# Layer-norm statistics of five tiles taken by ScalarE and GpSimd, and context statistics placed behind the scan

## The reference

```
x = x + attn(layernorm(x))          # 1024 -> 128, four layers, -> 1024
x = x + xattn(layernorm(x), ctx)    # top-k channel mask and pooling
x = x + ffn(layernorm(x))           # top 2 of 8 experts, 1024 x 1024 each

# attn, each layer: y = silu(ln(h)); y = sconv(y) (a complex recurrence over the
#   sequence); h = h + y*scale; y = ln(h); h = h + W2 silu(W1 y + b1) + b2
# xattn: mask = top 154 of 256 entries of ctx along the sequence, per channel
#   crucial = mask*x, rest = (1-mask)*x; max and mean of both over the sequence,
#   a 7-tap convolution over the channels, a norm, a sigmoid: two gates
#   out = crucial*gate1 + rest*gate2
# ffn: the two best experts per row, weighted with a softmax of their logits
```

## Time and profile before

| | |
|---|---|
| median of 3 runs | 1062.95 us (1062.17 to 1064.01) |
| the profiled execution | 1063.64 us, span 1061.8 us |
| mean granted TensorE clock | 0.964 |
| busy: TensorE, VectorE, ScalarE, GpSimd | 985.7, 537.7, 383.2, 463.1 us |
| block 1 | 0 to 351 us |
| pooling (block 3) | 353 to 441 us |
| gates, residual, routing | 441 to 538 us |
| expert products | 538 to the end |

### The profile page before, as it was taken

The page is one execution under the profiler, slowest core; times in us unless marked ns, Lnnn a source line. Parts: engine busy times, 40 slices in busy tenths (PEclk is TensorE's granted clock), DMA queues, the critical chain, the costliest instruction groups (busy, mean ns, idle before and its releaser), DMA issues. The chain is left out here.

```text
span 1061.8 us, 13204 instructions
## 1 busy us (share of the span) xinstructions
PE 985.7 (93%) x3508; PEld 518.5 (49%) x3515; DVE 537.7 (51%) x1547; ACT 383.2 (36%) x1032; POOL 463.1 (44%) x567
## 2 busy tenths in 40 slices
PE   6888999999999797999299999999999999999995
PEld 5786556566554453355144444444444444444442
DVE  5548899999988799789832111111111111111111
ACT  2436889899873487488300000000000000000000
POOL 3664766766750100087153344444434333333341
PEclk9989999999999898999579999999999999999997
DMA  7520120200004300037676643737346373463332
GB/s 290 173 75 1 51 91 11 90 1 2 1 1 159 140 21 1 1 141 285 253 259 192 211 106 79 237 79 237 77 132 175 68 230 72 107 205 79 79 79 40
DMA packets 38462, 120.25 MB, mean 113 GB/s; under 512 B 6220, under 2 KB 9351, under 8 KB 38408
## 3 DMA queue, kind: packets, MB, share of 16 engines
q1 hardware_dynamic: 25592, 79.77, 20.6%
q0 software_dynamic: 12816, 39.86, 16.8%
HBM read 82.91 MB, written 36.70 MB: 113 GB/s over the span
## 5 line engine op out<-in xcount | busy, mean ns | idle before, releaser
L2106 PE MATMUL bank<-T,X 128*128 x1184 | 510.2, 594 | 0.8 <-DVEq L2156 0.8
L2106 PEld LDWEIGHTS bank<-T,X 128*128 128x128 f32 x1184 | 225.6, 191 | 285.5 <-issue 285.5
L2154 DVE TENSOR_SCALAR X<-bank,col_p 128x512 f32<-128x512 f32 x37 | 27.8, 750 | 386.7 <-PE bank L2106 386.7
L2127 ACT ACTIVATE X<-bank,col_p 128x512 f32<-128x512 f32 x37 | 25.4, 687 | 493.8 <-PE bank L2106 493.8
L2066 POOL DMA_INDIRECT out_dram<-X,col_d x37 | 60.0, 1622 | 261.0 <-DVE X L2154 244.8
L2057 POOL DMA_INDIRECT X<-x_nrm,col_s x152 | 145.7, 959 | 51.3 <-issue 46.2
L490 POOL TENSOR_TENSOR rs<-ve,neg_half 128x4 f32<-128x4 f32 x36 | 52.9, 1470 | 55.1 <-DVE ve L979 55.1
L849 ACT ACTIVATE M<-X,T 128x256 bf16<-128x256 f32 x152 | 75.1, 501 | 0.0
L665 PE MATMUL bank<-nat,T 128*128 128x512 f32 x128 | 62.8, 612 | 3.4 <-DVE ve L979 2.0
L1502 DVE STREAM_TRANSPOSE X<-X 128x1024 f32<-128x1024 f32 x39 | 48.4, 1240 | 33.1 <-DMA X<-x_nrm,col_s 30.2
L673 PE MATMUL bank<-X,T 128*128 128x512 f32 x128 | 60.6, 602 | 0.0
(11 more groups left out here) (341 smaller groups left out, 1407.8 us busy)
## 6 DMA issues: line engine op xcount, KB each, us to landing
T<-in_L_ffn_expert_w_dram SPq DMA_DIRECT2D x8, 4096.0 KB, 17.6
out_dram<-X SPq DMA_DIRECT2D x17, 512.0 KB, 5.9
M<-in_x_dram SPq DMA_DIRECT2D x16, 512.0 KB, 7.6
X<-in_x_dram SPq DMA_DIRECT2D x16, 512.0 KB, 5.9
x_nrm<-H SPq DMA_DIRECT2D x16, 512.0 KB, 3.8
T<-in_ctx_dram SPq DMA_DIRECT2D x9, 512.0 KB, 3.6
X<-x_nrm,col_s POOLq DMA_INDIRECT x152, 3.7
X<-in_ctx_dram SPq DMA_DIRECT2D x4, 512.0 KB, 7.0
```

What stands on the lines that cost most here:

```text
L2106: mm = nc.tensor.matmul(bank[2 * u + n][:, :], xgt[u][:, k, :], Tf[:, ds(odd * D + (k * N + n * BANK), BANK)], start=(k == 0), stop=(k == ...
```

## The change

- **Statistics of tiles 0 to 4.** `rows` of these tiles now also sums each half row (`accum_out`). GpSimd makes the mean of the two sums (`squared_mean`); ScalarE squares the two halves of the row with the mean as its bias and sums them (`squared_tile`); GpSimd adds the two sums, multiplies by 1/1024 and adds epsilon (`squared_var`), then takes the power. All of this is in block 1. VectorE takes no statistics of tiles 0 to 4 any more, neither those of tiles 0 and 1 in block 1 nor those of tiles 2 to 4 in block 3.
- **Context statistics.** In slots up to 2 `stats` stands behind `scan` instead of at the head of the slot.
- Three semaphores are merged into others, the `spill` buffer is made earlier, and `sums` has one more wait, for the squares that wrote the same buffers.

```diff
         def counted(m, t):
-            return m * NT + t + 1 - (sum(...) if m == 1 else 0)
+            if m == 0:
+                return t + 1 - sum(i in SQUARED for i in range(t + 1))
+            return NT - len(SQUARED) + t + 1 - sum(on_scalar(*divmod(i, CT)) for i in range(t + 1))
...
         def rows(act, t):
             for n in range(2):
+                from_bank = bank[2 + 2 * (t % 2) + n][:, :]
+                if t in SQUARED:
+                    if SQUARED.index(t) >= 4:
+                        hold(act, sq_var, 2 * (SQUARED.index(t) - 4) + 2)
+                    hold(act, o2_mm, 2 * t + n + 1)
+                    nc.scalar.activation(X[:, t, n * BANK:(n + 1) * BANK], from_bank, ACT.Copy, accum_out=sum_at(t, n)).then_inc(x1_done, 1)
...
+        def squared_mean(pool, t):
+            pool.wait_ge(x1_done, 2 * t + 2)
+            nc.gpsimd.tensor_scalar(mean_of(0, t), sum_at(t, 0), sum_at(t, 1), 1.0 / D, ALU.add, ALU.mult).then_inc(sq_mean, 1)
+
+        def squared_tile(act, t):
+            k = SQUARED.index(t)
+            if k > 0:
+                hold(act, sq_sum, k)
+            hold(act, sq_mean, k + 1)
+            for n in range(2):
+                ins = nc.scalar.activation(wide_junk[n], X[:, t, n * BANK:(n + 1) * BANK], ACT.Square, scale=-1.0, bias=mean_of(0, t),
+                                           accum_out=sum_at(t, 2 + n))
+            ins.then_inc(sq_sum, 1)
+
+        def squared_var(pool, t):
+            k = SQUARED.index(t)
+            var = ve_all(0)[:, t:t + 1]
+            pool.wait_ge(sq_sum, k + 1)
+            nc.gpsimd.tensor_tensor(var, sum_at(t, 2), sum_at(t, 3), ALU.add).then_inc(sq_var, 1)
+            pool.wait_ge(sq_var, 2 * k + 1)
+            nc.gpsimd.tensor_scalar(var, var, 1.0 / D, EPS, ALU.mult, ALU.add).then_inc(sq_var, 1)
+            pool.wait_ge(sq_var, 2 * k + 2)
...  # GpSimd, end of block 1
-                for t in range(CT):
+                squared_mean(pool, 0)
+                for t in range(FIRST_TILES):
+                    if t + 1 < FIRST_TILES:
+                        squared_mean(pool, t + 1)
+                    squared_var(pool, t)
                     ln_pow(pool, 0, t)
...  # ScalarE, end of block 1
                 for t in range(FIRST_TILES):
                     rows(act, t)
+                    if t > 0:
+                        squared_tile(act, t - 1)
+                squared_tile(act, FIRST_TILES - 1)
...  # VectorE, a slot of block 1
-                    if b1 is not None:
+                    if b1 is not None and s > 2:
                         stats(b1, h1)
...
                     if 0 <= s + 1 < VISITS:
                         scan(s + 1)
+                    if b1 is not None and s <= 2:
+                        stats(b1, h1)
...  # VectorE, end of block 1
-                for t in range(CT):
-                    hold(dve, x1_done, 2 * t + 2)
-                    ln_stats(dve, 0, t)
...  # block 3: GpSimd, ScalarE's sums, VectorE
-                for t in range(CT, NT):
+                for t in range(FIRST_TILES, NT):
                     ln_pow(pool, 0, t)
...
+                    hold(act, sq_sum, sum(t < FIRST_TILES or t - 1 <= n + LAG + 1 for t in SQUARED))
...
-                    if CT <= t < NT:
+                    if t < NT and t not in SQUARED:
```

More of the change, by code:

```diff
@@ L217, in on_scalar, with sum_at @@
             return b >= FIRST_SQUARED and h == 0
+        SQUARED = list(range(FIRST_TILES))
         def counted(m, t):
-            return m * NT + t + 1 - (sum(on_scalar(*divmod(i, CT)) for i in range(t + 1)) if m == 1 else 0)
+            if m == 0:
+                return t + 1 - sum(i in SQUARED for i in range(t + 1))
+            return NT - len(SQUARED) + t + 1 - sum(on_scalar(*divmod(i, CT)) for i in range(t + 1))
+        def sum_at(t, k):
+            return back_of(0, 4 * (SQUARED.index(t) % 4) + k)
         def ln_stats(dve, m, t):
@@ L233, in ln_pow @@
         def ln_pow(pool, m, t):
-            pool.wait_ge(ln_var, counted(m, t))
+            if m == 1 or t not in SQUARED:
+                pool.wait_ge(ln_var, counted(m, t))
             nc.gpsimd.tensor_tensor(rstd_of(m, t), ve_all(m)[:, t:t + 1], neg_half[:, 0:1], ALU.pow).then_inc(ln_rstd, 1)
@@ L249, in rows @@
             for n in range(2):
-                hold(act, o2_mm, 2 * t + n + 1)
-                nc.scalar.copy(X[:, t, n * BANK:(n + 1) * BANK], bank[2 + 2 * (t % 2) + n][:, :]).then_inc(x1_done, 1)
+                from_bank = bank[2 + 2 * (t % 2) + n][:, :]
[4 more added lines that the diff above has]
+                    nc.scalar.activation(X[:, t, n * BANK:(n + 1) * BANK], from_bank, ACT.Copy, accum_out=sum_at(t, n)).then_inc(x1_done, 1)
+                else:
+                    hold(act, o2_mm, 2 * t + n + 1)
+                    nc.scalar.copy(X[:, t, n * BANK:(n + 1) * BANK], from_bank).then_inc(x1_done, 1)
+        spill = sb("spill", [P, CT, S], BF16)
+        wide_junk = [spill[:, :, :].rearrange("p k s -> p (k s)"), late[:, JUNK:JUNK + S].bitcast(BF16)]
+        sq_mean, sq_sum, sq_var = (sem(n) for n in ("sq_mean", "sq_sum", "sq_var"))
+        def squared_mean(pool, t):
[18 more added lines that the diff above has]
+            pool.wait_ge(sq_var, 2 * k + 2)
         VISITS = NL * CH
@@ L295, in decoder_kernel @@
         e_stat, e_mean, e_ve, e_rt, e_bc, e_bcs, e_h = (sem(n) for n in ("e_stat", "e_mean", "e_ve", "e_rt", "e_bc", "e_bcs", "e_h"))
-        wo_tp, wo_ev, wo_set, bo_mm = (sem(n) for n in ("wo_tp", "wo_ev", "wo_set", "bo_mm"))
+        wo_ev, wo_set = (sem(n) for n in ("wo_ev", "wo_set"))
         TABLE_STEPS = 1 + 11 * (NT // 2)
@@ L762, in _ @@
                             mm = nc.tensor.transpose(bank[t // 4][:, (t % 4) * P:(t % 4 + 1) * P], wo_raw[:, t * P:(t + 1) * P], ident[:, :])
-                        mm.then_inc(wo_tp, 1)
+                        mm.then_inc(set_pe, 1)
                     if s == -3:
@@ L767, in _ @@
                             mm = nc.tensor.matmul(bank[n][:, :], block_par[:, 2:3].to_broadcast([P, P]), wo_t[:, n * BANK:(n + 1) * BANK], start=True, stop=True)
-                        mm.then_inc(bo_mm, 1)
+                        mm.then_inc(set_pe, 1)
                     for p, step in prepared(s - 1):
@@ L898, in _ @@
                     if s == -4:
-                        act.wait_ge(wo_tp, 1)
+                        act.wait_ge(set_pe, 4)
                         for n in range(2):
@@ L1202, in _ @@
                     if s == -3:
-                        dve.wait_ge(bo_mm, 1)
+                        dve.wait_ge(set_pe, 5)
                         dve.wait_ge(ld_bout, 16)
@@ L1310, in decoder_kernel @@
         totals = logits[:, :, :].rearrange("p t e -> p (t e)")[:, 0:KD * B].rearrange("p (k b) -> p k b", k=KD)
-        spill = sb("spill", [P, KU // 2, S], BF16)
         junk = [spill[:, k, :] for k in range(2)] + [late[:, JUNK + k * S // 2:JUNK + (k + 1) * S // 2].bitcast(BF16) for k in range(2)]
@@ L1426, in decoder_kernel @@
         src_i = small(SLOTS, QK, dt=U32)
-        p_set, p_mm, r_fin = sem("p_set"), sem("p_mm"), sem("r_fin")
+        p_set, r_fin = sem("p_set"), sem("r_fin")
         n_weigh = [0]
@@ L1692, in _ @@
                                               start=(k == 0 and t == 0), stop=(k == 1 and t == NT - 1))
-                mm.then_inc(p_mm, 1)
+                mm.then_inc(r_pe, 1)
                 tile0.append(pe.value_load(ready_i[0:1, 0:1], min_val=1, max_val=E))
@@ L2164, in _ @@
                 v.tensor_scalar(dst_i[:, :], dst_f[:, :], -1.0, None, ALU.add)
-                dve.wait_ge(p_mm, 1)
+                dve.wait_ge(r_pe, 5)
                 weigh(dve, v.tensor_reduce(pair_p[:, :], bank[PROB][:, 0:3 * WIDE].rearrange("p (j s) -> p j s", j=3)[:, :, 0:SLOTS].rearrange("p j s -> p s j"), AX.X, ALU.add))
```

## The result

The changed kernel takes 1067.63 us, the median of its six runs, of which one (1586.08) fell in a slower state of the chip; the five others are 1066.09 to 1068.23 with a median of 1067.29. The kernel before has 1063.09 in the same comparison: ratio of the runs, without that one, 1.0035 [1.0024, 1.0046], slower by 3.7 us (the medians are 4.2 apart without it, 4.5 with it). Two more comparisons of the same two kernels gave 1.0030 [1.0018, 1.0042] and 1.0028 [1.0019, 1.0037]. The forecast was 1064.1 with a range to 1066.2, so it was wrong. It started from 1062.95, the median of three runs; in all 135 runs of the kernel before on record the median is 1063.9.

What follows compares the result with a forecast made beforehand. The prediction took a VectorE-GpSimd relay to bound block 1's end, and VectorE the pooling only from `crucial` of tile 2 (370.42). Tail +1.15, extra wait +0.05 and 0 elsewhere made +1.2 on 1062.95, about 1064.1; range 1061.2 to 1066.2.

Steps and rivals of the forecast that it cites:

- The tail, +1.15: End of block 1: squares of tiles 3 and 4 make GpSimd's last power start 1.15 us later.
- The early slots, 0: Context statistics moved behind the scan: slot 1 stalls go, slot 2 uses up the gain; sum 0, bounds -1.7 and +2.
- rival B: Early slots: VectorE's queue, not GpSimd's, holds slot 1, so 1.7 us is gained, time 1062.4; chance 0.12.
- Rival A: Slot 2: TensorE's longer gap at 117.28 halves its clock, +1.6 to +2 us, time 1065.9; chance 0.15.
- Rival D: End of block 1: longer tail, squares of 0.80, GpSimd's small operations 0.3 to 0.5, time 1064.8 to 1065.3; chance 0.10.
- The pooling, "17.4 us after the first normalized tile in both kernels": Block 3: `crucial` of tile 2 starts 17.4 us after the first normalized tile in both kernels, with TensorE's work and clock unchanged.
- Gain 0 from the removed statistics: Pooling: taking 5.4 us of statistics of tiles 2 to 4 off VectorE gains 0, bounds 0 and -0.3.
- Rival C: Pooling: `crucial` of tile 2 starts once VectorE is free, winning 4.2 us, time 1059.9; chance 0.08.
- The sum: Whole kernel: +1.15 + 0.05 + 0 = +1.2 us on 1062.95, about 1064.1; chance 0.55.

Runs made afterwards that it cites:

- e3: The kernel before with only tiles 0 and 1 by squares on ScalarE, context statistics not moved: 1061.02 us, ratio 0.9973.
- e7: The kernel before with only tiles 0 to 2 by squares on ScalarE, context statistics not moved: 1061.86 us, ratio 0.9979.
- e2: The kernel before with only the context statistics moved behind the scan in slots up to 2: 1064.27 us, ratio 0.9999.
- After_again: The changed kernel, unaltered, compared and profiled once more against the kernel before: 1066.19 us, ratio 1.0030.
- e1: The changed kernel without the move of the context statistics; five tiles still by squares: 1066.63 us, ratio 1.0025 to the kernel before.
- e4: The changed kernel with eight unused bf16 matmuls in TensorE's wait for the power of visit 1: 1066.82 us, ratio 1.0019 to the kernel before.
- e13: The changed kernel, unaltered, on the chip of e12, 12 runs beside 23 of the kernel before: 1066.63 us, ratio 1.0028.
- e14: The kernel before with unused matmuls on TensorE, 17 before and 4 behind the hand-over from block 1 to 3: 1063.17 us, ratio 0.9996.
- e11: The changed kernel with unused matmuls, 20 before and 4 behind the hand-over from block 1 to 3: 1063.18 us, ratio 0.9990 to the kernel before.
- e15: e11 again, on the chip of e14: 1063.28 us, ratio 0.9988 to the kernel before.
- e10: e3 with unused matmuls on TensorE, 2 before and 4 behind the hand-over from block 1 to 3: 1058.34 us, ratio 0.9949 to the kernel before.
- e9: The changed kernel with eight semaphore increments on VectorE ahead of its first tile of block 3: a single run, 1065.55 us.
- e6: e3 with unused matmuls on TensorE, 6 before and 6 behind the hand-over from block 1 to 3: 1059.90 us, ratio 0.9967 to the kernel before.
- e12: The kernel before with unused matmuls on TensorE, 14 before and 4 behind the hand-over from block 1 to 3: 1062.71 us, ratio 0.9993.

## Why the prediction was wrong

- *The tail, +1.15*: right. The last power is 1.14 further behind the flag, from the parts as predicted (0.71, 0.20, 0.28). As e3 and e7 show, it hangs wholly on tiles 3 and 4.
- *The early slots, 0*: right in the sum, to about 1 us, by e2. In the part, TensorE's wait in slot 2 grew to 1.65 and not to 2.7, because the prediction had nothing between the stall of 1.73 and that wait: ScalarE's copies, for which TensorE now waits 0.96, took most of it. After_again and e2 show the same (0.97, then 1.64) with GpSimd's power within 0.1 of where before has it (115.82, 115.79 and 115.90), so **rival B**'s gain didn't come. **Rival A** was right on what a fall near 118 costs, 1.7, and not shown on its cause: it comes with and without the move. The selection's end of 346.90 in after has such a fall in it, and the 346.69 of after_again has none; after had come to slot 2 1.5 earlier. **Rival D** didn't come: squares of 0.71, small operations 0.28 apart.
- *The pooling, "17.4 us after the first normalized tile in both kernels"*: **this step failed.** It was 18.33, and 17.79 to 18.23 in four more profiles with five squared tiles (e1, e4, e13, after_again). It took TensorE's clock for the same in both because the idle time ahead of it is long in both, but the clock's return varies by 3.1 us between executions of like work, worth 1.5 us, and it left out the later start of one VectorE instruction, 0.38. The first is chance, as far as the ten executions without added matmuls tell; the second is a term of the changed kernel.
- *Gain 0 from the removed statistics*: right where it was measured, but it holds only while the clock is down: at the full clock VectorE is last in the kernel before (e14). **Rival C** is real there, at 0.88 and not at 4.2, by one execution of each kind.
- *The sum.* The profiled pair adds up: flag 0.18, tail 1.14, clock 0.57, start 0.38, 2.27 of the 2.4 of span. Without chance, 1.14 + 0.38 = 1.5 is what the traces place. The three comparisons say 3.0 to 3.7. So half of the slowdown, and more than half of the miss, is not in any trace here. The three profiled executions of the changed kernel lie 1.2 below the median of its own runs, that of before 0.7 above the median it was shown with. What spreads the traced executions is known in part, and what is known of it is TensorE's clock: a fall near 118 (1.7), its return in block 3 (0.5 for each us), and the first us of the expert products, where e2 has it at 1.00 from 540 to 543 and after at 0.50 (508.4 and 510.2 us for the same 1184 matmuls). The runs without a trace have a mean granted clock on record too. It is 0.9638 over 21 runs of the changed kernel and 0.9667 over 129 of before, which is 6 us more at half clock (0.0029 of 1064 us, each us of half clock taking 0.5); the three traced ones have 0.963, 0.969 and 0.968. A half clock at a place where TensorE sets the pace would account for the rest at 0.5 us for each us. It would also fit that e11 and e15 lie 3.4 below the changed kernel where their traces show 1.9 to 2.4. At which place it lies, and why these kernels have more of it, isn't shown and stays open.
- *The range* had room for one cause at a time (A, or a longer tail). Two small costs with one sign, and a size known to 1 us from one execution, needed more above: 1067.6 is 1.4 outside (the median of the five other runs, 1067.3, is 1.1).

## What to carry to other kernels

Work moved off an engine only helps ahead of the point where that engine is last; here three tiles' statistics fit ahead of it, and the fourth and fifth put ScalarE and GpSimd behind it. Ask of each item in a batch, not of the batch, whether it lands before or behind the wait that closes a stage. And where TensorE idles for some microseconds ahead of a stretch that it paces, what the clock does there is a term with a spread; with two squared tiles a few matmuls of which nothing is used were worth about as much as the edit itself (5.4 in e10, 2.9 in e3).

## What the runs showed of the hardware

- At the hand-over from block 1 to block 3, TensorE's clock was at 0.50 after the idle stretches of 3.2 (e3) to 8.4 us (e9); with 1.79 to 2.42 of idle time left (e6, e10, e11, e14, e15) it stayed at 1.00, with 2.60 (e12) it fell. In the same kernel it fell 2.4 us into that idle stretch in one execution (after) and 4.8 in another (after_again). Near 118, where TensorE idles for 1.20 without the move and for about 1.64 with it, it fell in some executions of both. The Trainium skill, TensorE: Matmul & The Clock Gate, Part 1, has the clock follow how busy the array was of late; these traces agree, and add that two executions of like work differ by 3.1 us in when it comes back.
- The same VectorE instruction behind the same wait started 0.67 to 0.69 or 0.29 to 0.30 after its releaser ended; the later start came together with a packet of the instruction queue 0.60 to 0.90 behind it.
- A semaphore increment on VectorE cost about 0.1 us (eight moved the first normed tile from 7.46 to 8.21 behind the flag).
